# Moving the output weight's preparation behind the first exponentials in a fused cross-attention block

## The reference

```python
q = _ln(queries, q_norm_g, q_norm_b); kv = _ln(tokens, kv_norm_g, kv_norm_b)
qp = q @ in_proj_w[:D].T + in_proj_b[:D]            # and kp, vp from kv
scores = einsum('bhld,bhtd->bhlt', qh, kh) / sqrt(hd)
scores = scores - spatial_scale * dist + spatial_offset    # dist from two coordinates
attn = softmax(where(mask, scores, -inf))
x = queries + (attn @ vh) @ out_proj_w.T + out_proj_b
h = gelu(_ln(x, mlp_norm_g, mlp_norm_b) @ mlp_w1.T + mlp_b1)
x = x + (h @ mlp_w2.T + mlp_b2)
```

## Time and profile before

| | |
|---|---|
| median of 3 runs | 1236.29 us (1236.13 to 1237.63) |
| the profiled execution | 1237.08 us, of which 1235.3 us are the span from first to last instruction |
| TensorE busy | 1206.8 us, 98% of the span |
| VectorE, ScalarE, GpSimd busy | 934.4 us (76%), 876.9 us (71%), 999.3 us (81%) |
| mean granted TensorE clock | 0.998 of 2.4 GHz |

### The profile page before, as it was taken

How to read it: one execution, slowest core, us unless ns; L and a number is a source line. 1 busy time by engine, 2 the same in 40 slices (tenths; PEclk the granted TensorE clock), 3 DMA queues, 4 the chain that set the end, 5 groups by cost and what they waited for, 6 DMA issues and landing times.

```text
span 1235.3 us, 27472 instructions
## 1 busy us (share of the span) xinstructions
PE 1206.8 (98%) x9320; PEld 788.7 (64%) x9320; DVE 934.4 (76%) x2467; ACT 876.9 (71%) x2062; POOL 999.3 (81%) x1287
## 2 busy tenths in 40 slices
PE   7899899999999999999999999999999999999998
PEld 3444466766666676666666666666666666666664
DVE  5799997888787787888787787888777777667321
ACT  6899777777767676777768776777767776776331
POOL 5698999989898989989897989989898988777320
PEclk9999999999999999999999999999999999999999
DMA  8599998999989898989998997988999898788433
GB/s 245 166 239 198 257 214 187 205 212 180 208 197 210 202 216 181 207 213 179 207 190 212 202 221 182 207 209 185 207 194 207 198 217 172 162 179 177 140 118 121
DMA packets 469181, 241.62 MB, mean 196 GB/s; under 512 B 384672, under 2 KB 409392, under 8 KB 469040
## 3 DMA queue, kind: packets, MB, share of 16 engines
q1 hardware_dynamic: 469040, 239.86, 86.0%
HBM read 109.66 MB, written 12.58 MB: 99 GB/s over the span
## 4 chain that ended last, share of the span: by engine, by line
PE 84%; POOL 5%; DVE 4%; ACT 3%; issue 2%; DMA 1%; SPq 1%; POOLq 0%; DVEq 0%; ACTq 0%
PE ps_down L690 26%; PE ps_up L675 26%; PE ps_qk L610 11%; PE ps_vo L634 6%; PE ps_vo L631 6%; PE ps_s L646 4%; PE ps_pv L660 4%; POOL soft L1346 1%; POOL p_nat L1338 1%; DVE soft L1132 1%; POOL soft L1329 1%; ACT soft L842 1%; DMA w_stage<-in_w_qkv 1%; POOL raw L1296 0%; ACT ps_down L786 0%
## 5 line engine op out<-in xcount | busy, mean ns | idle before, releaser
L675 PE MATMUL ps_up<-hT,w 128*128 128x256 f16 x3072 | 377.2, 273 | 1.4 <-ACT u L889 1.3
L690 PE MATMUL ps_down<-w,hid 128*128 128x512 f16 x1536 | 372.9, 379 | 0.6 <-DVE hid L1182 0.4
L675 PEld LDWEIGHTS ps_up<-hT,w 128*128 128x128 f16 x3072 | 300.4, 98 | 90.8 <-ACT u L889 1.7
L1338 POOL TENSOR_SCALAR p_nat<-soft,row_inv 128x256 f16<-128x256 f32 x480 | 297.7, 630 | 61.3 <-DVE row_inv L1140 59.1
L842 ACT ACTIVATE soft<-soft,neg_max 128x256 f32<-128x256 f32 x512 | 255.2, 500 | 120.3 <-DVE neg_max L1132 119.5
L1132 DVE CUSTOM_DVE_ANT_0 soft<-ps_s,soft,factor 128x256 f32<-128x256 f32 x512 | 225.8, 477 | 143.2 <-PE ps_s L646 142.9
L1150 DVE SCALAR_TENSOR_TENSOR p_nat<-soft,row_inv,p_nat 128x256 f16<-128x256 f32 x480 | 268.4, 599 | 2.6 <-POOL p_nat L1338 2.6
L1346 POOL TENSOR_SCALAR soft<-dist,scale_neg,offset 128x512 f32<-128x512 f32 x256 | 248.1, 969 | 11.8 <-DVE p_nat L1150 10.0
L889 ACT ACTIVATE u<-ps_up,bias,up_scale 128x256 f32<-128x256 f32 x256 | 142.5, 557 | 135.7 <-PE ps_up L675 135.6
L690 PEld LDWEIGHTS ps_down<-w,hid 128*128 128x128 f16 x1536 | 148.6, 97 | 132.0 <-DVE hid L1182 1.1
L1354 POOL TENSOR_SCALAR hid<-u,hid_scale 128x1024 f16<-128x1024 f32 x64 | 82.1, 1282 | 101.6 <-ACT u L895 101.0
(11 more groups left out here) (135 smaller groups left out, 1574.5 us busy)
## 6 DMA issues: line engine op xcount, KB each, us to landing
w<-x_scratch SPq DMA_DIRECT2D x256, 256.0 KB, 3.1
stack<-qk_parts SPq DMA_DIRECT2D x256, 96.0 KB
raw<-in_ctx SPq DMA_DIRECT2D x32, 256.0 KB, 3.5
raw<-in_x SPq DMA_DIRECT2D x32, 256.0 KB, 3.0
c_stage<-in_w SPq DMA_DIRECT2D x16, 512.0 KB, 5.0
x<-in_x SPq DMA_DIRECT2D x32, 256.0 KB, 3.5
out<-x SPq DMA_DIRECT2D x32, 256.0 KB, 3.3
tok_rows<-in_tok_xy SPq DMA_DIRECT2D x16, 256.0 KB, 3.8
```

What stands on the lines that cost most here:

```text
L675: mm = e.matmul(ps_up[s % 2][:, 0:L], w_1_sb[:, wp, k, m * P:(m + 1) * P], hT[:, b % 2, :, xp * KT + k, :], start=(k, wp, xp) == (0, 0, 0) ...
L690: mm = e.matmul(ps_down[tt][:], hid[:, chunk % HID_RING, i, hp, tt * P:(tt + 1) * P], w_2_sb[:, s % W2_RING, wp, :], start=(m == 0 and (hp ...
L1338: mine = e.tensor_scalar(p_nat[:, nat, HI, lc, :], soft[:, ring, lc, :], row_inv[:, ring, lc:lc + 1], 1.0, ALU.mult, ALU.mult)
```

## The change

Five steps move by one slot or two, and no instruction is added, removed or resized.

- ScalarE: the value's row copy (`bias_row`) goes from slot -2 to slot 0, the Square of W_o (`weight_square`) from -2 to 0, the squares of the pieces 2 and 3 of W1's first chunk from -2 and -1 to 0. In slot 0 all of them stand behind `exps(0)`. W_o's HI parts, before two in slot 1 and two in slot 2, all stand in slot 2.
- TensorE: `total(3)` and `total(4)` go from slot 0 to slot 1, behind `qk_project` of that slot.
- VectorE: `square_norm(3)` goes from slot 0 to 1, `gains(3)` from 1 to 2, W_o's LO parts from slots 1 and 2 to slots 2 and 3. `square_norm(4)` and `gains(4)` stay in slots 1 and 2.
- GpSimd: `norm_root(3)` goes from slot 0 to 1.
- SP: the value's `bias_turn` goes from slot -1 to 1, where it stands ahead of `stack_copies(1)`.

```diff
-        TOTAL = (-30, -28, -4, 0) + tuple(range(0, 32, 4))
-        NORM = (-28, -25, -3, 0) + tuple(range(1, 33, 4))
-        GAIN = (-27, -24, -3, 1) + tuple(range(2, 34, 4))
+        TOTAL = (-30, -28, -4, 1, 1) + tuple(range(4, 32, 4))
+        NORM = (-28, -25, -3, 1) + tuple(range(1, 33, 4))
+        GAIN = (-27, -24, -3, 2) + tuple(range(2, 34, 4))
...
-                for sec, at_slot in ((SEC_K, -25), (SEC_Q, -24), (SEC_V, -1)):
+                for sec, at_slot in ((SEC_K, -25), (SEC_Q, -24), (SEC_V, 1)):
                     if slot == at_slot:
                         bias_turn(sec)
...
-                for sec, at_slot in ((SEC_K, -26), (SEC_Q, -24), (SEC_V, -2)):
+                for sec, at_slot in ((SEC_K, -26), (SEC_Q, -24), (SEC_V, 0)):
                     if slot == at_slot:
                         bias_row(sec)
...
-                for half_of in due(slot, 1, ITEM, 2):
-                    weight_hi(SEC_O, range(2 * half_of, 2 * half_of + 2))
+                if slot == 2:
+                    weight_hi(SEC_O, range(KT))
...
-                for sec, at_slot in ((SEC_V, -6), (SEC_O, -2)):
+                for sec, at_slot in ((SEC_V, -6), (SEC_O, 0)):
                     if slot == at_slot:
                         weight_square(sec)
...
+                if slot == 0:
+                    for k in (2, 3):
+                        chunk_square(0, k)
                 for step in due(slot, -4, ITEM, 2 * N_CHUNKS * KT):
-                    chunk_square(*divmod(step, KT))
+                    if step not in (2, 3):
+                        chunk_square(*divmod(step, KT))
...
-                for half_of in due(slot, 1, ITEM, 2):
+                for half_of in due(slot, 2, ITEM, 2):
                     weight_lo(SEC_O, range(2 * half_of, 2 * half_of + 2))
```

## The result

| | changed | before, run beside it |
|---|---|---|
| median, first set (8 runs each) | 1241.35 us | 1236.89 us |
| ratio, 95% interval | 1.003 [1.002, 1.004] | |
| median, second set (11 and 31 runs) | 1241.56 us | 1237.81 us |
| ratio, 95% interval | 1.0028 [1.0019, 1.0037] | |

The change costs 0.3%, 3 to 4.5 us. 1238.5 was forecast, with a range up to 1240.5: the sign is that of the sum, the size isn't. The 1236.29 that I started from was also at the lower end of what the kernel before takes: on that scale the second set's ratio would give 1239.8, inside the range.

What follows compares the result with a forecast made beforehand. The bound was taken as a chain from VectorE's early slots through the transposes to TensorE, which never stops from 188.75 us. VectorE's added waits of 2.2 us on 1236.3, all else zero, gave 1238.5 us, range 1235.2 to 1240.5.

Steps and rivals of the forecast that it cites:

- ScalarE's idle 2.2 us: Ahead of qk_hi(1,1), ScalarE stands idle 2.2 us for TensorE's projection, so exps(0) comes only about 1.9 earlier.
- Both totals wait 1.1: In slot 1, TensorE waits 1.1 us for ScalarE's squares at total(3) and another 1.1 at total(4).
- VectorE's waits: Up to the maxima of item 4, VectorE's idle time grows from 5.32 to 7.58 us, 2.26 more, taken as 2.2.
- Handed on: The whole 2.2 us at slot 4 passes through VectorE and the transposes to the end; 0.4 either way.
- absorbed: Rival: a parallel path is the real limit after slot 4, so the 2.2 us vanish: 1236.3 us; chance 0.20.
- The clock falls: Rival: TensorE drops to the 1.2 GHz level after a new wait, 1.24 us more, 1239.7 us; chance 0.05.
- The longest new wait: TensorE's longest new wait was put at 1.9 us, at scores(5).
- the likeliest one: Case in which VectorE's 2.2 us at slot 4 carry through to the end: 1238.5 us; chance 0.49.
- Faster: Rival: squares are ready at the totals in slots 0 to 4, TensorE's waits of 2.8 us go: 1233.5; chance 0.12.
- collision: Rival: delayed transposes issued at 66.25 meet other transfers, 2.0 us more, 1240.5 us; chance 0.12.
- drain: Rival: ScalarE's table load ahead of exps(0) also costs its drain, 1.4 us more, 1239.9 us; chance 0.02.
- The start of the count: The median of the kernel before, 1236.3 us, to which the forecast added 2.2.

Runs made afterwards that it cites:

- the filled pair: Kernel before and changed kernel, both with matmuls without a use at TensorE's waits behind slot 2, the changed one also at both totals: 1236.65 and 1239.57 us.
- the parts alone: Kernel before with only W_o's parts moved, all HI parts to slot 2, LO parts to slots 2 and 3: 1240.03 us, ratio 1.0016.

## Why the prediction was wrong

**ScalarE's idle 2.2 us: right.** 2.10, exps(0) at 40.37, and the one line that puts the Square into it removes the loss from the runs.

**Both totals wait 1.1: right**, 1.26 and 1.01.

**VectorE's waits: right as a sum of waits**, 7.62 against 7.58 where the clock doesn't fall ahead of them. The step "its list of work up to the maxima of item 4 is the same before and after, so the start of those maxima moves by the change in idle time" was short: the work is the same, its duration isn't. Term mis-sized: 0 forecast, 0.7 measured in the kernels with fillers, of which 1.07 is the LO parts of W_o and the rest steps that got longer and shorter. The waits' 2.3 and these 0.7 are the 3.0 at item 5; the runs of the filled pair show 2.7.

**Handed on: right for the filled pair**, which keeps 2.9 of 3.0 to the last long wait and 2.7 in the runs, so "absorbed" fell for it. For smaller delays the runs don't show it: with the Square back 1.2 and, filled, 1.3 us at item 5 came out as -0.4 and 0.3 between the means of the runs taken together, each uncertain by about 0.8.

**The clock: wrong, and this is the failing step.** The rival "The clock falls" held single waits against single waits, 1.9 against the 2.10 and 5.06 of one execution. The fall came behind 1.26 and 1.01 with 0.35 us of matmuls between. The longest new wait wasn't 1.9 either: in the two profiles where the clock stays up to there, with fillers at the totals and with the Square back, it is 2.15, ahead of item 4. And one execution can't give a safe side: the kernel with the parts alone fell behind 0.40 and 1.01, and in the changed kernel's profile the wait of 2.09 at 137.59 has a fall behind it, where 2.10 at 133.19 had none before. I also set the clock as a case beside the likeliest one, with a chance of 0.05, where the two add up: 2.2 + 1.24 would have been 3.4 as the likeliest. The Trainium skill (TensorE: Matmul & The Clock Gate, "A second HAM failure mode: psum-queue depth-cycling") tells of a kernel in which frequent small idle gaps between groups of matmuls make the clock go up and down. The trace agrees in that the fall stands behind two waits close together, total(4) 1.84 for 1.02; that the same thing is at work isn't shown. What the prediction names, the Trainium skill's "HAM oscillation" (TensorE: Matmul & The Clock Gate), is about a kernel that stops for DMAs for longer than any new wait here, and alone it gave no reason to fear waits as short as these.

**What the clock costs.** The fall is seen in the rows; its price isn't known closely. In the changed kernel's two profiles item 5's scores are 24.1 and 23.4 behind qk(1,1), against 22.4 with fillers at the four waits: 1.6 and 1.0 by the early fall. In the runs, unfilled 3.1 between the means, filled 2.7, filled at four waits 2.3: a share of 0.4 to 0.8, each difference uncertain by about 0.8, and the pair with fillers in the prologue has 3.8, no share at all. By the other way, the mean clock is 0.0015 lower, and over all runs a thousandth goes with 0.6 us: 0.9. About 0.4 to 1.0, then, and not settled: the runs alone don't rule out zero.

**Faster, collision, drain: fell.** Squares were ready at 45.6, not 43.0; the x transposes took 3.68 (3.82); exps(0) followed the table load by 0.01.

**The start of the count.** The 1236.29 of three runs was low. The medians of 8 to 33 runs of the same kernel are 1236.9 to 1238.2, 0.6 to 1.9 higher; against the run beside it the ratio is what the change is to be judged by. The 2.9 us between 1238.5 and the first 1241.35 are therefore 0.6 of this start, some 0.5 of durations (2.7 for 2.2), 0.4 to 1.0 of clock, and for the rest most likely chance, as the first set's medians are 4.5 apart and all runs' means 3.1.

Left open: why the parts alone (1.0016) cost anything in the runs and nothing with the Square back. The fall of the clock in the profile of the parts alone, 1.6 us, is part of it; how often it falls there isn't known, and the effect on GpSimd and VectorE together wasn't taken apart.

## What to carry to other kernels

Before work is moved out of an engine's way, look at what the freed engine will wait for: here 4.0 us of work stood ahead of an instruction whose input was 2.2 away, and the piece that just fills that gap (the Square, 1.9) should have stayed. A wait of TensorE has to be looked at together with the waits close to it, and in more than one execution; what a fall of the clock costs came here on top of the critical path's delay. An instruction's duration is not a constant: when VectorE's instructions move, ask what GpSimd does beside them there. And take the start of the count from more than three runs.

## What the runs showed of the hardware

- The same kernel runs at a mean clock of 0.991 to 0.999 from one execution to the next, and from 1235.3 to 1243.3 us with it. Fillers at twelve places from slot 3 to slot 37 raised the mean clock from 0.9953 to 0.9975 and cut the mean by 1.4 us, beside 29 runs of the kernel before. With fillers at the two totals alone, the one profile has the fall at the next wait.
- An LO part of W_o (two inputs and the output in SBUF, 128x512) took 0.75 us in the kernel before and up to 1.14 beside GpSimd's tile work. By line and tile, from the changed kernel with the fillers:

```profile
L1078 DVE SCALAR_TENSOR_TENSOR w_o<-w_stage,factor,w_o x4: 748/1094/1135, 49.7 to 55.2; 128x512 f16<-128x512 f32 x4
```

GpSimd's instructions at that time are slower too: its 128x512 copy took 0.93 (0.62 in the kernel before), the bias tile 1.19 (0.77):

```profile
50.39 0.93 POOL L1324 TENSOR_SCALAR x_nat<-raw 128x512 f16<-128x512 f32 x1
51.31 1.19 POOL L1357 TENSOR_SCALAR soft<-dist,scale_neg,offset 128x512 f32<-128x512 f32 x1
```

Work side by side doesn't always slow VectorE: in the changed kernel's first profile the second pair of LO parts took 1.40 at 57.97, and there it is GpSimd's bias tile at 58.15 that took 2.36 instead of 0.77. The Trainium skill (GPSIMD Engine Reference, "1. Specifications") names an SBUF interface that GpSimd shares with VectorE's instructions of two SBUF inputs. The rows agree with it; no run here separates it from another cause.
